# A three-layer graph network on one core: where in layer 0 the counts' store and the work on layer 2's weights stand

## The reference

```python
def _mean_agg(x, src, dst, n):
    msg_sum = segment_sum(x[src], dst, num_segments=n)
    cnt = segment_sum(ones((src.shape[0], 1)), dst, num_segments=n)
    return msg_sum / maximum(cnt, 1.0)
def _sage_conv(x, src, dst, Wl, bl, Wr):
    return _mean_agg(x, src, dst, n) @ Wl.T + bl + x @ Wr.T
h = maximum(_layernorm(x), 0.0)
g = relu(_batch_norm(_sage_conv(h, ...), gamma0, beta0))
g = relu(_batch_norm(_sage_conv(g, ...), gamma1, beta1))
g = _sage_conv(g, ...)
return x + log_softmax(g, axis=-1)
```

## Time and profile before

| | |
|---|---|
| median of 3 runs | 1426.08 us (1422.99 to 1427.76) |
| profiled execution | 1434.69 us, span 1432.8 us |
| granted TensorE clock | 0.995 of full speed |
| busy: TensorE, VectorE, ScalarE, GpSimd | 1335.7, 582.0, 511.1, 563.9 us |
| layer 0 | to about 543 us of the span |

### The profile page before, as it was taken

How to read it: one execution, slowest core, us unless ns; L and a number is a source line. 1 busy time by engine, 2 the same in 40 slices (tenths; PEclk the granted TensorE clock), 3 DMA queues, 4 the chain that set the end, 5 groups by cost and what they waited for, 6 DMA issues and landing times.

```text
span 1432.8 us, 31432 instructions
## 1 busy us (share of the span) xinstructions
PE 1335.7 (93%) x13653; PEld 836.9 (58%) x13653; DVE 582.0 (41%) x1081; ACT 511.1 (36%) x848; POOL 563.9 (39%) x562
## 2 busy tenths in 40 slices
PE   1389999999998999999999999999999999999997
PEld 0277878787777887664444444444447754444445
DVE  5977877777879852120111112011102212221223
ACT  4786878887887863420000000000000510000001
POOL 3423242414051000006666666666661026666650
PEclk9999999999999999999999999999999999999999
DMA  6155555646464561356665666666651688988983
GB/s 167 37 187 170 178 192 174 206 156 217 170 220 157 193 222 44 139 187 215 225 209 204 226 229 228 222 224 208 206 187 61 212 297 298 319 320 305 314 306 100
DMA packets 113589, 291.15 MB, mean 203 GB/s; under 512 B 19938, under 2 KB 55412, under 8 KB 113412
## 3 DMA queue, kind: packets, MB, share of 16 engines
q1 hardware_dynamic: 85196, 228.74, 45.9%
q0 software_dynamic: 21824, 55.44, 12.5%
q10 hardware_dynamic: 6424, 4.88, 1.1%
HBM read 197.78 MB, written 91.22 MB: 202 GB/s over the span
## 4 chain that ended last, share of the span: by engine, by line
PE 74%; DMA 7%; ACT 6%; issue 5%; DVE 4%; POOL 3%; SPq 0%; another core or an unknown queue 0%; ACTq 0%; DVEq 0%; POOLq 0%
PE cells L1650 33%; PE bank L1223 13%; PE bank L1650 6%; PE cells L1215 5%; PE cells L1716 3%; POOL hots L548 3%; ACT ring L684 3%; DMA hots<-table,src_i 3%; PE cells L1256 2%; PE cells L1653 2%; PE cells L1728 2%; DMA rc_row<-cntg 1%; PE bank L1903 1%; PE cells L1903 1%; DVE hots L909 1%
## 5 line engine op out<-in xcount | busy, mean ns | idle before, releaser
L1650 PE MATMUL cells<-ring,parts 128*128 128x500 f16 (+1 forms) x2548 | 643.2, 373 | 0.0
L548 POOL DMA_INDIRECT hots<-table,src_i x444 | 422.2, 951 | 455.6 <-DMA table<-parts 218.4
L1650 PEld LDWEIGHTS cells<-ring,parts 128*128 128x128 f16 (+1 forms) x2548 | 239.1, 96 | 284.7 <-issue 19.4
L684 ACT CAST ring<-cells 128x980 f16<-128x980 f32 (+1 forms) x325 | 329.8, 1070 | 85.8 <-PE cells L1215 62.4
L1223 PE MATMUL bank<-ring,parts 128*128 128x250 f16 (+1 forms) x2450 | 296.5, 272 | 6.1 <-DVE agm L918 4.8
L909 DVE TENSOR_TENSOR hots<-iotas,tab 128x980 f16<-128x980 f16 (+3 forms) x262 | 248.4, 999 | 19.1 <-PE cells L1215 14.8
L1223 PEld LDWEIGHTS bank<-ring,parts 128*128 128x128 f16 (+1 forms) x2450 | 226.5, 98 | 38.0 <-issue 8.6
L1650 PE MATMUL bank<-ring,parts 128*128 128x500 f16 (+1 forms) x490 | 183.5, 374 | 0.0
L755 ACT ACTIVATE agmg<-cells,isp 128x124 f32<-128x124 f32 x16 | 5.8, 365 | 454.8 <-PE cells L1265 454.8
L1215 PE MATMUL cells<-hots 64*128 64x49 f16 x4670 | 95.2, 186 | 35.1 <-DVE hots L909 29.1
L1215 PEld LDWEIGHTS cells<-hots 64*128 64x128 f16 x4670 | 76.0, 95 | 70.6 <-issue 34.1
(11 more groups left out here) (211 smaller groups left out, 1042.3 us busy)
## 6 DMA issues: line engine op xcount, KB each, us to landing
ring<-c_blocks SPq DMA_DIRECT2D x120, 750.0 KB
c_blocks<-ring SPq DMA_DIRECT2D x175, 437.5 KB
ring<-c_blocks SPq DMA_DIRECT2D x40, 812.5 KB
rcb<-rc_row SPq DMA_DIRECT2D x69, 125.0 KB
hots<-table,src_i POOLq DMA_INDIRECT x444
Z<-in_x_dram SPq DMA_DIRECT2D x4, 768.0 KB, 7.3
table<-parts SPq DMA_DIRECT2D x2, 1536.0 KB
table<-parts ACTq DMA_DIRECT2D x2, 1536.0 KB
```

Source lines behind the costliest of these rows:

```text
L548: pool.indirect_dma_start(out=got[layer][:, 5 * (r % NGOT) + i, :], out_offset=None, in_=tables[layer], in_offset=bass.IndirectOffsetOnAxi ...
L684: act.copy(blk[c % 2][:, :, :].rearrange("p a (d g) -> p a d g", d=GD)[:, :, :, GPS * i:GPS * i + n], cells[t % NCELL][:, :, 0:n * NA].rea ...
L1650: ins = pe.matmul(bank[b][:, 0:2 * BD].rearrange("p (s d) -> p s d", s=2), lhs, ring[0:r, :, BD * a:BD * a + BD], start=(a, part) == (0, 0 ...
```

## The change

SyncE's loop in layer 0 now issues the piece of a step before the counts' store of that step (both fall on step 9). On VectorE three calls stand elsewhere: dve_norms(1) moves from (21, 3) to (21, 5), dve_spread(1) from (22, 9) to (23, 0), dve_spread(2) from (23, 9) to (24, 0).

```diff
@@ sync_layer0
                     what, q, _ = chores.get(t, ("", 0, 0))
-                    if what == "count":
-                        counts_store(q)
                     if c >= 1 and t - NST * c in piece_at:
                         a0, a1 = pieces[piece_at[t - NST * c]]
                         sp.wait_ge(a_cells, min(t, NST * NB))
                         sp.dma_start(C_dram[c - 1, :, :].rearrange("p (a n) -> p a n", n=BD)[:, a0:a1, :],
                                      blk[(c - 1) % 2][:, a0:a1, :]).then_inc(d_store[(c - 1) % 2], 16)
+                    if what == "count":
+                        counts_store(q)
@@ dve_layer0
-                    elif (c, i) == (NB - 4, 3):
+                    elif (c, i) == (NB - 4, 5):
                         dve_norms(1, own)
                     elif (c, i) == (NB - 4, 8):
                         dve_absolute(2, own)
-                    elif (c, i) == (NB - 3, 9):
+                    elif (c, i) == (NB - 2, 0):
                         dve_spread(1, own)
-                    elif (c, i) == (NB - 2, 9):
+                    elif (c, i) == (NB - 1, 0):
                         dve_spread(2, own)
```

## The result

The changed kernel takes 1415.21 us (median of 6 runs, 1412.46 to 1417.17), the kernel before 1423.94 us in 6 runs beside it (1421.74 to 1427.76): ratio 0.9929 with a 95% interval of 0.9910 to 0.9948, 7.4 to 12.8 us faster. The forecast was 1419.7 us, range 1415.5 to 1424.5, and 6.4 us of gain. In three later comparisons the same change gave 0.9953, 0.9977 and 0.9967, so its size is itself something to explain.

What follows compares the result with a forecast made beforehand. TensorE, busy for 93% of the span, was taken to bound the kernel, so only its idle time could be won. Store's order 3.7 + norms 2.7 + spreads 0 = 6.4 us off the median 1426.08: 1419.7 us, range 1415.5 to 1424.5.

Steps and rivals of the forecast that it cites:

- the list of gaps: TensorE's gaps in layer 0 behind blocks 1, 9 and 13, plus its 3.0 us wait in block 21, to be won.
- Part 1, the store's order: At six block boundaries, the last piece going ahead of the counts' store shortens ScalarE's wait; 3.7 us, bounds 2.3 to 3.8.
- the terms 0.67, 0.34 and 1.1: TensorE's gaps behind block 1 that the store's order gives back, in us; 1.1 is taken of a 1.20 gap.
- The terms 0.29 and 1.27: TensorE's gaps behind block 9 (0.29 us) and block 13 (1.27 us) that the store's order gives back.
- Part 2, norms: In block 21, moving dve_norms(1) behind the mean removes TensorE's 3.0 us wait; 2.7 us net, bounds 2.0 to 3.0.
- The 0.3 us taken off for block 22: The mean in block 22 would come 0.3 us late for TensorE, so the norms' gain was 3.0 − 0.3.
- Spreads: Moving dve_spread(1) and (2) ends VectorE idle time but gains 0; a margin of 1.3 to 1.5 us stays in block 23.
- The sum and its base: 3.7 + 2.7 = 6.4 us, from a profiled execution of 1434.69 us, taken off the median 1426.08: 1419.7 us.
- the forecast case: The 6.4 us gain arrives, own range 5.0 to 7.5 us, 1417 to 1423 with the spread of medians; chance 0.64.
- the first (only the norms): Only the norms' part arrives, the store's order wins nothing for TensorE: −2.7 us, 1423.4 us; chance 0.15.
- The second (issue gaps take the gain back): TensorE's own issue gaps open in the vacated stretches, 4 to 5 us come back: −2 us, 1424; chance 0.12.
- The fourth (SyncE held too long): Counts' store round trip above some 15 us makes the next block's seventh piece late at six boundaries: 1436 us; chance 0.04.

Runs made afterwards that it cites:

- e8: Kernel before the change, with each batch's counts' store done twice so the last piece goes out later; ratio 1.0222 (1.0194 to 1.0251), +31.5 us.
- e1: Kernel before the change, with only the last piece moved ahead of the counts' store; ratio 0.9974 (0.9959 to 0.9990), −3.7 us.
- e4: Kernel before the change, unchanged, run again for a second trace; ratio 0.9991 (0.9974 to 1.0007).
- e2: Kernel before the change, with only dve_norms(1) moved to (21, 5); ratio 0.9969 (0.9954 to 0.9985), −4.4 us.
- e16: Kernel before the change, unchanged, run on chip 13 for its trace; ratio 1.0001 (0.9984 to 1.0018).
- e3: Kernel before the change, with only dve_spread(1) and (2) moved, to (23, 0) and (24, 0); ratio 1.0001 (0.9982 to 1.0020).
- e14: Kernel before the change, with the store's order alone changed, run on chip 13; ratio 0.9991 (0.9976 to 1.0007).
- e6: Changed kernel with both spreads put back where they were; ratio to the kernel before 0.9963 (0.9945 to 0.9980).
- e5: Changed kernel, unchanged, beside new runs of the kernel before; 1414.58 against 1420.42 us, ratio 0.9953 (0.9938 to 0.9969).
- e9: e7 with the mean at step 2 also in block 2 and dve_norms(0) at (20, 6), on chip 13; ratio to the kernel before 0.9994.
- e7: Changed kernel with the mean at step 2 in blocks 4, 8, 12, 16, 20, 24; ratio to before 0.9913, 1408.97 us; 0.9982 on chip 13.

## Why the prediction was wrong in its number

**What bounds the kernel, and the list of gaps:** the kind of gap was right, the list only in part. The gaps behind block 1 are in the traces of before and go with the store's order. The 1.27 us of block 14 is in the one trace alone: the block lasts 19.2 us there and 17.3 to 17.4 in every other trace, of either order, but that of e8, which lengthens the wait.

**Part 1, the store's order, 3.7 us:** the mechanism was right, and the number agrees with e1 (3.7 us, interval 1.4 to 5.8), in part by luck. In the traces the stretch behind the first boundary shrinks from between 39.7 and 40.7 us to between 37.9 and 38.2, some 2.1 us and what the terms 0.67, 0.34 and 1.1 say. The terms 0.29 and 1.27 found no gap to remove in e4. ScalarE's wait shrank as forecast (0.8 us, once; 0.9 in e1), and the slack of 2.3 us holds at four of six boundaries (e8). The sentence that weighed the 2.0 us plus bytes over 436e3 of the Trainium skill ("DMA: Bandwidth & Descriptors", Anatomy of one DMA) also held: the counts' store kept SyncE for 4.8 to 6.4 us in the changed kernel too.

**Part 2, norms, 2.7 us:** the mechanism was right, the term too small; e2 measured 4.4 us (2.1 to 6.5, which takes in 2.7), and block 21 is 4.4 us shorter in its trace than in that of e4. Two corrections are seen. The 0.3 us taken off for block 22 never came as a wait, since VectorE was 0.7 us further ahead of TensorE in block 21 than in the trace that I had read (it reached the place of the norms at 440.78, 1.0 us before the linear part at 441.79; before it was 451.68, 0.3 ahead of 451.96). And the 3.0 us wait has a tail that I did not price. The 15 products behind it take 1.77 us in the earlier trace rows but here, in the second execution of before:

```profile
447.73 3.18 PE L1223 MATMUL bank<-ring,parts 128*128 128x250 f16 x15 [3.00 <-DVE agm L918]
```

3.18 us, 1.4 more; 3.29 and 2.94 in e1 and e16, 1.77 in e3 and e14. Without the wait they take 1.79 (after). The tail is TensorE's clock. In the same stretch of e4 and then of the earlier trace rows, the number behind the last bracket (0.53, then 1.00) is the granted clock:

```profile
447.73:450.84 3.11, 3.11 (x15) 2.06 (x16) 3.11 (x3) 0.00 (x0) 0.00 (x0) 0.53 0.00 0
```

```profile
457.29:459.00 1.71, 1.71 (x15) 1.36 (x17) 1.71 (x2) 0.00 (x0) 0.00 (x0) 1.00 0.00 0
```

It is 0.53 in e4, 0.50 in e1 and 0.57 in e16, mostly the lower of its two levels (1.2 of 2.4 GHz), and 1.00 in the first trace of before, in e3 and in e14, behind the same 3.0 us of idleness. So the wait costs 3.0 or 4.4 us: block 21 lasts 20.6 us in these three, 22.0 to 22.1 in e1, e4, e8 and e16, and 17.6 or 17.7 in nine of the ten traces with the norms moved. The prediction read it off an execution of the cheaper kind.

**Spreads, 0:** right (e3, e6), with the margin forecast in block 23 never used.

**The sum and its base:** this is the step that failed. It reads: "Its surplus doesn't sit in these gaps so far as I can see, so I take the same 6.4 from the median". The traces contradict it. A second execution of the same kernel (e4) is 8.2 us shorter in layer 0, and 1.9 of these are block 14 with the gap of 1.27 that the sum counts. The term for the norms failed in the other direction: 2.7 us in the sum, 4.4 by e2 and by block 21 in e4. By the traces of e1, e2 and e4, an estimate of the gain is 2.1 + 4.4 = 6.5 us (5.1 where the clock stays up), where the prediction has 3.7 + 2.7 = 6.4 and e5 measured 6.7. The total was right there because two errors cancel, and that is luck.

What carries 1415.21 out of the range is in part not in the sum at all. Of the 4.5 us between 1419.7 and 1415.21, 2.1 are the base (1426.08 in three runs, 1423.94 in six) and 2.3 the gain (8.7 by the medians against 6.4). The ratio's 10.1 us there and the 6.7 of e5 lie within the intervals, which share 7.4 to 8.8 us. I did not find a cause for the larger gain of the first comparison beyond its spread, and it stays open.

**The range:** its lower end of 1415.5 rested on 1417 for the forecast case. It held no case in which the first median was high, and in which the norms won more than their wait.

**Rivals:** the first (only the norms) is refuted by e1, whose interval is clear of 1. The second (issue gaps take the gain back) is seen on the chip of e9 to e16 in the block shown, and not in the layer as a whole. The fourth (SyncE held too long) had round trips of 4.8 to 6.4 us against its 15 and never came near.

## What to carry to other kernels

A wait of a helper engine is worth what is left above the slack of the engine behind it. Read the slack from several boundaries, or lengthen the wait on purpose, as e8 did: 1.5 to 3.8 us were free here, boundary by boundary. What is above may cost more than itself, since TensorE's clock can be lower behind the gap (0.53 of full speed behind 3.0 us of idleness in e4): read the granted clock there, and price the wait by the length of the block. When independent work stands ahead of an instruction that the bounding engine waits for, put the latter first; the same move in five more blocks (e7) was worth as much again. Before a trace's gaps are summed, compare the profiled time with the median: a surplus of 8.6 us in one execution means that some gaps may belong to the execution, and a second trace of the unchanged kernel would have told which: here one of the gaps in the sum. And an edit that wins 12 us on one chip and 3 on another (e7) has to be timed on both before it is called better: e7 is ahead of both kernels on the first and only equals the change on the second.

## What the runs showed of the hardware that was not expected

TensorE has stretches in blocks 3, 7, 11, 15 and 19, near the indirect loads of the windows' ends (L521), in which four or five cell products take 0.25 us and 0.5 us of issue follow, several times over. They appear in all traces of some groups of runs (7.6 to 11.1 us in e9 to e16, 6.2 in the first trace of before) and in none of the others (e1 to e8, at most one of 0.6 us). In e4 the same loads run (187.28 to 193.16 us, block 7) and no such gap follows. They do not go with the kernel. All traces with 7.6 us or more are of one chip by the record (13), so chip, time and state are not told apart; the chip of the first trace of before is not on record. Where they are absent TensorE waits for the mean instead (7.8 to 13.0 us in those with the mean at step 4), so part of them covers waits that exist anyway. What feeds them (the supply of instructions competing with transfers would be one guess) was not tested and stays open. On that chip layers 1 and 2 are also longer: 895.2 us from L1855 to the end in e16 against 883.2 in e4, with 15.6 against 6.0 us of waits for the gathered rows.

The same 3.0 us of idleness, behind 5 us without a break, left TensorE's granted clock at 1.00 in three traces (the first of before, e3, e14) and between 0.50 and 0.57 over the next 15 products in three others (e1, e4, e16). Behind waits for the mean of 2.01 us or less, 15 products take 1.77 us in every trace that has such a wait; behind one of 2.04 they take 2.12 (after), and behind the waits of 2.6 to 3.4 us in block 4 they take 2.4 to 3.2. What decides in a single case is not shown here.
